# Patch attention that projects x itself, two tiles summed by VectorE, and null-key output products spread over the eighth pair of heads

## What is computed

```python
x = x + _L0_xattn_ref(...); x = x + _L0_ffn_ref(...); x = x + _L1_xattn_ref(...)
x = x + _L1_ffn_ref(_layernorm(x, axis=-1), ...)     # gated attention
x = x + _L2_xattn_ref(_layernorm(x, axis=-1), ...)   # patch attention
x = x + _L2_ffn_ref(_layernorm(x, axis=-1), ...)     # sorted experts
x = x + _L3_xattn_ref(_layernorm(x, axis=-1), ...)   # null-key attention
x = x + _L3_ffn_ref(_layernorm(x, axis=-1), ...)     # sparse experts
```

```python
# L1_ffn, end: 8 heads, 8 experts; the outputs of the experts are weighted and summed
out = jnp.einsum('bshep,hepd->bsd', weighted, o_w.reshape(H, E, P, D))
# L2_xattn: only the first term depends on x
h = rmsnorm(embeds, g_res)                     # embeds is the layer-normalised x
h = jnp.einsum('bld,ed->ble', h, W_in) + b_in
return depool_out + h                          # depool_out comes from the context
# L3_xattn, end: 16 heads of 64, one null key and value in front of 256 keys
out = jnp.einsum('bhij,bhjd->bhid', attn, v)
out = out.transpose(0, 2, 1, 3).reshape(b, -1, INNER)
out = jnp.einsum('bnf,fd->bnd', out, Wout)
out = (out - mu) * jax.lax.rsqrt(var + EPS) * ln_scale + ln_bias
```

## Time and profile before

| | us |
|---|---|
| median of 3 runs | 1215.19 |
| lowest and highest of them | 1213.39, 1217.17 |
| the profiled execution | 1217.53 |
| its span, first to last instruction | 1216.0 |
| TensorE busy | 1052.8 |
| VectorE busy | 812.4 |
| ScalarE busy | 663.5 |
| GpSimd busy | 388.6 |
| mean granted TensorE clock | 0.914 |

### The profile page before, as it was taken

One profiled execution on the slowest core, in us unless ns is written; L12 is line 12 of the kernel. 1 busy time (PEld: TensorE's weight loads), 2 busy tenths in 40 slices (PEclk: granted clock), 3 DMA queues, 4 the chain that ended last, 5 costly groups with the idle time before them and its releaser, 6 DMA issues.

```text
span 1216.0 us, 18098 instructions
## 1 busy us (share of the span) xinstructions
PE 1052.8 (87%) x5940; PEld 734.3 (60%) x5940; DVE 812.4 (67%) x1982; ACT 663.5 (55%) x1635; POOL 388.6 (32%) x613
## 2 busy tenths in 40 slices
PE   3587899999958999878899999996699899997777
PEld 2345677777732333655677767774567576765665
DVE  5764688877857856358787876766755666665463
ACT  3253567676632757456677787875134466665121
POOL 5221112111111101034565656757300344444200
PEclk8687799999975969989899999998699899999879
DMA  6502000000023510030000000121500100000000
GB/s 217 107 21 92 1 1 14 1 1 1 1 65 104 180 40 3 2 138 1 1 0 1 2 1 1 53 87 31 219 1 2 71 2 1 2 1 2 1 1 18
DMA packets 26572, 45.08 MB, mean 37 GB/s; under 512 B 3536, under 2 KB 23792, under 8 KB 25200
## 3 DMA queue, kind: packets, MB, share of 16 engines
q1 hardware_dynamic: 23936, 41.57, 10.0%
q10 hardware_dynamic: 2544, 2.36, 0.6%
HBM read 36.94 MB, written 6.82 MB: 36 GB/s over the span
## 4 chain that ended last, share of the span: by engine, by line
PE 42%; DVE 9%; ACT 8%; issue 3%; POOL 2%; DMA 1%; SPq 0%; DVEq 0%; ACTq 0%; POOLq 0%
PE psum L1735 7%; ACT region_d L1801 4%; PE psum L2384 3%; PE psum L2352 2%; PE psum L2336 2%; PE psum L2319 2%; ACT region_c L1818 2%; PE psum L1772 2%; PE psum L2314 2%; PE psum L1749 2%; PE psum L409 1%; PE psum L2395 1%; PE psum L2730 1%; PE psum L2311 1%; PE psum L1053 1%
## 5 line engine op out<-in xcount | busy, mean ns | idle before, releaser
L1735 PE MATMUL psum<-gated_parts 128*128 128x512 f32 x768 | 198.6, 411 | 15.1 <-DVE region_d L1905 10.9
L1735 PEld LDWEIGHTS psum<-gated_parts 128*128 128x128 f32 x768 | 141.4, 191 | 68.1 <-DVE region_d L1905 30.6
L1978 POOL TENSOR_TENSOR region_d<-region_d 128x256 f32<-128x256 f32 x128 | 100.8, 788 | 114.5 <-DVE region_d L1905 114.0
L1434 ACT ACTIVATE rounds_work<-psum,region_c 128x512 f32<-128x512 f32 x128 | 87.0, 689 | 59.2 <-PE psum L1349 59.2
L787 DVE TENSOR_REDUCE work<-psum 128x1 f32<-128x512 f32 x128 | 82.0, 686 | 33.0 <-PE psum L365 31.4
L1359 PE MATMUL psum<-parts,split 128*128 128x512 f32 x384 | 97.5, 403 | 0.0
L1801 ACT ACTIVATE region_d<-psum,gated_work 128x128 f32<-128x128 f32 x256 | 75.7, 452 | 36.7 <-issue 26.2
L1349 PE MATMUL psum<-parts,split 128*128 128x512 f32 x384 | 94.1, 395 | 0.0
L1504 DVE TENSOR_TENSOR parts<-rounds_work,parts 128x1024 fp32r<-128x1024 f32 x64 | 77.5, 1223 | 19.9 <-POOL parts L1590 17.4
L1590 POOL CAST parts<-rounds_work 128x1024 fp32r<-128x1024 f32 x32 | 33.3, 1042 | 179.4 <-ACT rounds_work L1434 179.4
L1905 DVE SCALAR_TENSOR_TENSOR region_d<-psum,gated_work,region_d 128x128 f32<-128x128 f32 x256 | 71.4, 344 | 28.7 <-ACT region_d L1801 15.0
(11 more groups left out here) (423 smaller groups left out, 2189.8 us busy)
## 6 DMA issues: line engine op xcount, KB each, us to landing
region_a<-in_l1v SPq DMA_DIRECT2D x1, 4096.0 KB, 14.7
region_b_last<-in_l1o SPq DMA_DIRECT2D x1, 4096.0 KB, 12.5
region_a<-in_l2f SPq DMA_DIRECT2D x1, 4096.0 KB, 13.5
region_b_last<-in_l3f_small SPq DMA_DIRECT2D x1, 4096.0 KB, 19.7
region_a<-in_l3f SPq DMA_DIRECT2D x1, 2080.0 KB, 7.4
region_c<-in_l0f SPq DMA_DIRECT2D x1, 2076.0 KB, 12.2
region_c<-in_l3x SPq DMA_DIRECT2D x1, 2048.0 KB, 7.6
ctx_parts<-front_work SPq DMA_DIRECT2D x6, 256.0 KB, 3.1
```

What stands on the lines that cost most here:

```text
L1434: act.activation(H[g % 2][:, f, :], bank[f], ACT.Gelu_apprx_tanh, bias=W("b1")[:, (g % E) * FT + f:(g % E) * FT + f + 1]).then_inc(h_ready ...
L1735: ins = pe.matmul(bank[2 * (n % 2) + c], src[a][:, t * P:(t + 1) * P], weights[b][:, piece(c)], start=m == 0, stop=m == len(PASSES) - 1)
L1978: pool.tensor_tensor(tile[:, 0:2, :], tile[:, 0:2, :], tile[:, 2:4, :], ALU.add).then_inc(k.pool_chain, 1)
```

## The change

There are four edits.

1. Gated attention: GpSimd stops after tile 125. VectorE, once it has merged tiles 126 and 127, adds both at once in three instructions of 512, 256 and 256 elements, the last onto x.
2. Patch attention: x is transposed as it is, half by half, as soon as its half is complete. The mean is taken out by the weights: GpSimd makes the matrix `centre` (identity minus 1/128), ScalarE scales w by `g_res`, one matmul multiplies the two and ScalarE copies the product. The inverse root is applied by VectorE in the last sum, which reads the matmul's result, the rstd and `xz` (x + z, made by GpSimd in two halves). The normalised tiles go away. The statistics stay.
3. Null-key attention: in turn b of the eighth pair TensorE does the output products of the first seven pairs for the two tiles of batch b, 14 matmuls. As they add to banks 6 and 7 without a start flag, ScalarE clears the two banks first, with two activations of 128x512 at the end of the seventh pair. The transposes of the null weights and their copy are split into two halves. Behind the last turn stand 8 output products of the eighth pair and 8 of the null values, and 4 of the 8 transposes.
4. The norms at its end: VectorE does statistics and `yn` of both halves, then x of both halves, then the next stage's norm for both halves (`Norm.vector`), where it had done the whole of it for one half and then the other.

The count of `norm2.ready` in the sorted experts is adapted.

```diff
--- before.py
+++ after.py
@@ -1075,7 +1075,7 @@
     def scalar(act):
         bank = k.bank
         k.norm.scalar(act, use, k.xnT)
-        act.wait_ge(k.norm2.ready, 2 * NT)
+        act.wait_ge(k.norm2.ready, NT)
         act.activation(xl_part[0], xl, ACT.Copy).then_inc(xl_high.semaphore, 1)
         act.activation(ident, k.ident[:, :], ACT.Copy).then_inc(ident_ready.semaphore, 1)
         act.activation(ident16, k.ident[:, :], ACT.Copy).then_inc(ident_ready.semaphore, 1)
@@ -1653,6 +1653,7 @@
     og = [k.carve(F32, NT, E) for _ in range(2)]
     den, NM, rec = k.carve(F32, 2, NT), k.carve(F32, NT), k.carve(F32, NT)
     BLOCKS = 2 * NH
+    LAST_TWO = BLOCKS * NT - 2
     PASSES = ((0, 0), (0, 1), (1, 0))
     GATE_GROUPS = (slice(0, 1), slice(1, 4), slice(4, 6), slice(6, 8))
@@ -1958,7 +1959,15 @@
             if h < NH:
                 denominators(h)
                 low_outputs(h)
-        dve.wait_ge(k.x_tiles, NT * (number + 1))
+        assert LAST_TWO % RING == RING - 2
+        two = free_d[:, (RING - 2) * HALF_E * P:RING * HALF_E * P].rearrange("p (r a n) -> p r a n", r=2, a=2)
+        last = k.x[:, NT - 2:NT, :]
+        dve.wait_ge(merged, LAST_TWO + 2)
+        chain.then(dve.tensor_tensor(two[:, :, 0, :], two[:, :, 0, :], two[:, :, 1, :], ALU.add))
+        chain.then(dve.tensor_tensor(two[:, :, 0, 0:P], two[:, :, 0, 0:P], two[:, :, 0, P:2 * P], ALU.add))
+        dve.wait_ge(summed, NT * (NH - 1))
+        dve.wait_ge(k.x_tiles, NT * number + NT // 2)
+        dve.tensor_tensor(last, last, two[:, :, 0, 0:P], ALU.add).then_inc(k.x_tiles, 2)
     def gpsimd(pool):
         k.norm.gpsimd(pool, use)
@@ -1971,7 +1980,7 @@
             pool.tensor_tensor(x_part[1][:, piece(c)], k.xnT[:, piece(c)], x_part[0][:, piece(c)].bitcast(F32), ALU.subtract)\
                 .then_inc(x_low.semaphore, 1)
         outputs = 0
-        for n in range(BLOCKS * NT):
+        for n in range(LAST_TWO):
             block, t = n // NT, n % NT
             tile = scaled[n % RING]
             pool.wait_ge(merged, n + 1)
@@ -2170,45 +2179,80 @@
     k.carve_from(REGION_B)
-    xr = k.carve(F32, NT, D)
-    xrT = k.carve(F32, T)
+    xz = k.carve(F32, NT, D)
+    xT = k.carve(F32, T)
+    scaled_w = k.carve(F32, P)
+    centre = k.carve(F32, P)
+    centred_w = k.carve(F32, P)
+    centre_ready = k.count("packed_normed", 1)
+    scaled_ready = k.count("packed_part", 1)
+    w_psum = k.count("packed_out_psum", 1)
+    w_ready = k.count("packed_wide_ready", 1)
+    turned, T_ready = k.norm2.turned, k.norm2.T_ready
     out_psum = k.sem(f"{name}_out_psum")
-    ahead_added = k.sem(f"{name}_ahead_added")
+    xz_ready = k.sem(f"{name}_xz_ready")
     def out(t):
-        return k.bank[4 + t % 4][:, 0:P] if t % 4 < 2 else k.bank[t % 4][:, 0:P]
+        return k.bank[4 + t // 4][:, (t % 4) * P:(t % 4 + 1) * P]
+    def half_of_x(engine, h):
+        engine.wait_ge(k.x_tiles, NT * (number - 1) + NT // 2 * (h + 1))
     def tensor(pe):
-        k.norm2.tensor(pe, 0, xr, banks=(6, 7))
-        pe.wait_ge(k.weights[name], 16)
+        half_of_x(pe, 0)
+        for t in range(4):
+            ins = pe.transpose(k.bank[6][:, t * P:(t + 1) * P], k.x[:, t, :], k.ident[:, :])
+        ins.then_inc(turned, 1)
+        pe.wait_ge(*centre_ready.at(1))
+        pe.wait_ge(*scaled_ready.at(1))
+        pe.matmul(k.bank[5][:, 0:P], centre, scaled_w, start=True, stop=True).then_inc(w_psum.semaphore, 1)
+        half_of_x(pe, 1)
+        for t in range(4):
+            ins = pe.transpose(k.bank[7][:, t * P:(t + 1) * P], k.x[:, 4 + t, :], k.ident[:, :])
+        ins.then_inc(turned, 1)
+        pe.wait_ge(*w_ready.at(1))
         for t in range(NT):
             if t % 4 == 0:
-                pe.wait_ge(k.norm2.T_ready, t // 4 + 1)
-            if t >= 4:
-                pe.wait_ge(k.x_tiles, NT * number + t - 3)
-            pe.matmul(out(t), xrT[:, t * P:(t + 1) * P], W("w"), start=True, stop=True).then_inc(out_psum, 1)
+                pe.wait_ge(T_ready, t // 4 + 1)
+            ins = pe.matmul(out(t), xT[:, t * P:(t + 1) * P], centred_w, start=True, stop=True)
+            if t % 4 == 3:
+                ins.then_inc(out_psum, 1)
     def scalar(act):
         act.wait_ge(k.weights[name], 16)
-        k.norm2.scalar(act, 0, xrT, banks=(6, 7), scale=W("g_res"))
+        half_of_x(act, 0)
+        act.activation(scaled_w, W("w"), ACT.Copy, scale=W("g_res")).then_inc(scaled_ready.semaphore, 1)
+        act.wait_ge(turned, 1)
+        act.activation(xT[:, 0:HALF], k.bank[6], ACT.Copy).then_inc(T_ready, 1)
+        act.wait_ge(*w_psum.at(1))
+        act.activation(centred_w, k.bank[5][:, 0:P], ACT.Copy).then_inc(w_ready.semaphore, 1)
+        act.wait_ge(turned, 2)
+        act.activation(xT[:, HALF:T], k.bank[7], ACT.Copy).then_inc(T_ready, 1)
     def vector(dve, chain):
-        k.norm2.vector(dve, chain, 0, k.x, xr, 1e-5, twice=True)
+        for h in range(2):
+            half_of_x(dve, h)
+            k.norm2.statistics(dve, chain, 0, k.x, 1e-5, False, h, twice=True)
         for t in range(NT):
             if t % 4 == 0:
-                dve.wait_ge(ahead_added, t // 4 + 1)
-            dve.wait_ge(out_psum, t + 1)
-            dve.tensor_tensor(k.x[:, t, :], k.x[:, t, :], out(t), ALU.add).then_inc(k.x_tiles, 1)
+                dve.wait_ge(xz_ready, t // 4 + 1)
+                dve.wait_ge(k.norm2.rstd_ready, t // 4 + 1)
+                dve.wait_ge(out_psum, t // 4 + 1)
+            dve.scalar_tensor_tensor(out=k.x[:, t, :], in0=out(t), scalar=k.rstd[:, t:t + 1], in1=xz[:, t, :],
+                                     op0=ALU.mult, op1=ALU.add).then_inc(k.x_tiles, 1)
         dve.wait_ge(k.x_tiles, NT * (number + 1))
     def gpsimd(pool):
-        k.norm2.gpsimd(pool, 0)
+        pool.tensor_scalar(centre, k.ident[:, :], -1.0 / D, None, ALU.add).then_inc(centre_ready.semaphore, 1)
         pool.wait_ge(ahead.z_ready, 2)
         for h in range(2):
             half = slice(4 * h, 4 * h + 4)
-            pool.wait_ge(k.norm2.ready, 4 * h + 4)
-            pool.tensor_tensor(k.x[:, half, :], k.x[:, half, :], ahead.z[:, half, :], ALU.add).then_inc(ahead_added, 1)
+            half_of_x(pool, h)
+            pool.tensor_tensor(xz[:, half, :], k.x[:, half, :], ahead.z[:, half, :], ALU.add).then_inc(xz_ready, 1)
+            k.norm2.power(pool, 0, h)
     def sync(sp):
         sp.wait_ge(k.x_tiles, NT * number)
@@ -2294,6 +2338,7 @@
     ent_sb = sem("ent_sb")
     out_psum = sem("out_psum")
     x_biased = sem("x_biased")
+    cleared = k.count("experts_cwT_sb", 2)
     def tensor(pe):
         bank = k.bank
@@ -2352,6 +2397,20 @@
                     ins = pe.transpose(bank[4 + g % 2][:, kt * S + t * P:kt * S + (t + 1) * P],
                                        PR[g % 4][:, t, kt * P:(kt + 1) * P], k.ident[:, :])
             ins.then_inc(pt_psum, 1)
+        def output(t, pairs):
+            for p in pairs:
+                pe.matmul(bank[6 + t // 4][:, (t % 4) * P:(t % 4 + 1) * P], oT[p][:, t * P:(t + 1) * P], W("o")[:, p, :],
+                          start=False, stop=True, skip_group_check=True)
+        def turn_null_weights(h):
+            pe.wait_ge(exp_ready, ITEMS * PAIRS)
+            pe.wait_ge(prob_ready, ITEMS * (PAIRS - 1) + 4 * h + 4)
+            for t in range(4):
+                ins = pe.transpose(bank[h][0:HEADS, t * P:(t + 1) * P], EN[:, 4 * h + t, :], k.ident[:, :])
+            ins.then_inc(ent_psum, 1)
         for i in range(3):
             project(0, i)
@@ -2376,6 +2435,13 @@
                 if p + 1 < PAIRS:
                     for c in MADE_IN[b]:
                         project(p + 1, c)
+                else:
+                    pe.wait_ge(*cleared.at(b // 2 + 1))
+                    pe.wait_ge(av_sb, B * (PAIRS - 2) + b + 1)
+                    for t in range(TPB):
+                        output(TPB * b + t, range(PAIRS - 1))
+                    if b == B - 1:
+                        turn_null_weights(0)
                 pe.wait_ge(pt_sb, g + 2)
                 if b % 2 == 0:
                     pe.wait_ge(proj_sb, len(CHUNKS) * p + 5 + b // 2)
@@ -2385,19 +2451,17 @@
                                         PT[(g + j) % 4][:, kt, :], start=kt == 0, stop=kt == TPB - 1,
                                         tile_position=(0, j * DH))
                 ins.then_inc(av_psum, 1)
-        for t in range(NT):
-            ins = pe.transpose(bank[t // 4][0:HEADS, (t % 4) * P:(t % 4 + 1) * P], EN[:, t, :], k.ident[:, :])
-        ins.then_inc(ent_psum, 1)
-        pe.wait_ge(av_sb, B * PAIRS)
-        for t in range(NT):
-            dst = bank[6 + t // 4][:, (t % 4) * P:(t % 4 + 1) * P]
-            for p in range(PAIRS):
-                pe.matmul(dst, oT[p][:, t * P:(t + 1) * P], W("o")[:, p, :], start=p == 0, stop=False)
-            if t == 0:
-                pe.wait_ge(ent_sb, 1)
-            ins = pe.matmul(dst, ENT[0:HEADS, t * P:(t + 1) * P], NVW[0:HEADS, :], start=False, stop=True)
```

(41 more changed lines are left out.)

## The result

Twenty runs of the changed kernel have a median of 1205.47 us (1200.11 to 1214.32), twenty of the kernel before 1218.34. The ratio is 0.9898, 95% interval 0.988 to 0.9917: 12.4 us faster, 10.1 to 14.6. The forecast was 10.1 us and a median of 1205.1 us.

What follows compares the result with a forecast made beforehand. TensorE, busy 87% of the span, was taken to bound most stages, so gains lie where it waits. 6.5 us (gated and patch attention) + 3.6 us (null-key attention) = 10.1 us: median 1205.1, range 1201 to 1209.

Steps and rivals of the forecast that it cites:

- Part 1: Gated attention's end: with VectorE adding the last two tiles, x is whole at 844.65 instead of 847.40, 2.75 us earlier.
- Part 2: Patch attention: without normalised rows in the chain, x is complete at 851.4; with the gated attention's edit 6.5 us gained.
- Part 3: Null-key attention, eighth pair: output products fill TensorE's waits, so the last product ends at 1139.0 instead of 1144.95.
- 72 matmuls ... 0.266 us each: Null-key attention: price of output products, 1125.8 to 1144.95; 14 per turn add 3.72 us, making a turn 6.7 us.
- the 6.38 us of gaps: Eighth pair's turns: TensorE's waits, 3 x 1.62 + 0.58 + 0.94 us, all taken to go.
- Clearing: End of the seventh pair: two added ScalarE activations delay the eighth pair's transposes, taken as 0.2 us.
- Part 4: Norms ending the null-key attention: 10.7 us follow the last product, giving back 2.4 of 6.0 us gained by early products.
- the filler is hidden: Eighth pair: added products hide the turn's chain; the rival, each turn 4.6 + 3.7 us and 1211.5 in all, had 0.07.
- the patch chain's limit: Patch attention: TensorE's second-half matmuls end last; rival, a queue counted as hidden limits, gain 3.2 us, 1208.4, chance 0.07.
- the slower case: Rival, eighth pair to last product: TensorE granted 1.2 GHz over 32 us of matmuls, up to 1237 us; chance 0.04.
- a turn of 6.6 to 6.9 us: Sign that the forecast is right: each turn of the eighth pair takes 6.6 to 6.9 us.
- The course of the clock: Rival: TensorE's fall in granted clock at 960 to 970 vanishes (1202.0) or one more is added (1208.2); chance 0.16.

Runs made afterwards that it cites:

- second experiment: The kernel before with the patch attention's edit alone, GpSimd still summing all tiles: ratio 0.9987 to the kernel before.
- eighth experiment: The changed kernel with the first four tiles' last products, null values, sums and statistics ahead of the second half's: ratio 0.9873 to the kernel before.
- experiment 4: The kernel before with the new order of the norms alone, output products as before: ratio 1.0051 to the kernel before.
- fifth experiment: The changed kernel with each tile's last output product followed at once by its null value's product, not four and four: ratio 0.9958 to the kernel before.
- seventh experiment: The changed kernel with the patch attention's centred weights made during the gated attention and GpSimd's sums ahead of its powers: ratio 0.9917 to the kernel before.

## Why the prediction was right or wrong

- **Part 1.** Forecast: x whole 1.81 us behind the merge, measured 1.91. GpSimd's two adds for tile 125 lost 0.57 us (0.97 and 0.51) beside VectorE's, forecast 0.66, and GpSimd's next work was late by that and no more. The Trainium skill (GPSIMD Engine Reference, Key points) says that GpSimd shares its SBUF interfaces with VectorE and contends with its instructions that have two SBUF inputs; the trace agrees, with 0.97 us beside such an add and 0.46 elsewhere.
- **Part 2.** Forecast: x complete 8.6 us behind the merge, measured 8.7, with TensorE at 1.2 GHz (granted 0.50 from 842 to 846) and its second half last, as forecast. That the sum held is in part luck. Centring took 0.72 us against 0.3 (0.55 in the second experiment, where no add of VectorE ran beside it). GpSimd starting 0.16 sooner and the product and the transposes taking 1.44 instead of 1.70 made up for it, so that the eight matmuls started 3.81 us behind the merge instead of 3.76. Parts 1 and 2 together: forecast 6.5, measured 6.33.
- **Part 3, the step that failed.** "72 matmuls ... 0.266 us each": the mean of 0.222 for a product and some 0.6 for a null value with its two changes of shape. The turn was 6.08 instead of 6.7, and grouping the null values by four, which I priced at nothing, took away 12 of the 16 changes at 0.193, 2.3 us. With these prices the run of before is 72 x 0.222 + 16 x 0.193 = 19.1 us, as measured, and a turn 2.98 + 14 x 0.222 = 6.1. The last product came 29.43 us into the stretch instead of 31.65. A second slip hid behind the surplus: of the 6.38 us of gaps only 5.80 went, as the fourth turn's 0.58 stayed, 0.57 us at 1116.68. The filler stands behind the transposes that this gap precedes, and I had counted it all the same. Clearing cost 0.19 as forecast (0.2). Put together, 37.60 - 5.80 - 2.3 + 0.19 = 29.7; the 0.3 us that are left I have not taken apart. No run puts other work into the fourth turn's gap; the eighth experiment kept it, too. The same step held a warning that I turned around: that the 0.266 included changes was taken as a reason that changes are cheap.
- **Part 4.** 10.7 us behind the last product forecast, 10.85 measured; experiment 4 had 10.79. Giving back 2.4 of part 3's gain is confirmed by experiment 4. That the norms' new order is nevertheless worth 2.61 us behind early products I had not said: the text compared it only with the old order behind late ones.
- **Sum.** 6.33 + 5.71 = 12.04 us in the stretches against 10.1, the surplus from part 3. The timed ratio gives 12.4, its interval reaches to 10.1. That the median of 1205.47 lies beside the forecast of 1205.1 is luck: the forecast started from three runs with a median of 1215.19, and twenty have 1218.34, so a base 3.1 us too low met a gain 2.3 us too small.
- **Rivals.** No turn waits ahead of its attention products, so the filler is hidden; the patch chain's limit was the one named; the granted clock stayed at 1.00 from 1097.6 to 1127.0, the dense stretch, so the slower case did not occur. Of the signs named, a turn of 6.6 to 6.9 us failed with part 3. The course of the clock did shift by some us elsewhere, in both directions, as allowed for.

## What to carry to other kernels

Work put into a loop pays by the gaps that come behind it in the engine's order, and only if the stage behind the loop does not then take longer: the worth of an order of the tail (which half first) turned from +2.4 to -2.6 us with when its inputs came, so price such edits together. A mean over a mixed run of instructions is not a price; take it apart by shape before the mix is changed, since grouping like matmuls was worth 2.3 us here, beside 5.8 from the gaps. Where a chain behind the last result waits on small steps, look for what does not need the result, as the transposes of x here, and then for which engine's instruction order is next.

## What the runs showed of the hardware

- A change between matmuls with 128 and with 16 rows cost 0.193 us at full clock, a mean of both directions, nearly as much as a 128x128 product's 0.222 (changed kernel and fifth experiment).
- A `tensor_scalar` from SBUF to SBUF on VectorE, 0.17 us alone, took until the end of a two-input add that GpSimd had in progress: 0.44 (842.54) and 1.16 us (844.21) in the changed kernel, 1.15 in the seventh experiment. `bn_stats` beside the same adds kept its 0.86. Where an add of VectorE with two SBUF inputs and one of GpSimd ran side by side, both were longer: 0.56 and 0.50 us for 256 elements on VectorE (0.42 alone, line 2894 at 1143.80), 0.97 instead of 0.46 for 128 on GpSimd.
- TensorE was granted the lower clock for 8.9 us of unbroken work at one place in the changed kernel's profile and for 3.7 at the same place in that of before. In the fifth experiment it was granted the full clock up to a wait of 0.45 us and the lower one in the matmuls of alternating shape behind it (0.57 over the 6 us).
